# Flamingo block on one core: the last absorbed queries in another PSUM bank, and three steps of the second attention issued in another order

## The reference

```python
x = x + tanh(g_xattn[1]) * attention(layernorm(x), ctx_512, ...)

def attention(hidden_q, kv_c, Wq, w_kc_q, w_kc_kv, W_qr, W_kr, Wo):   # 16 heads, 1444 keys of 64
    q_big = rope(einsum('bshk,hkq->bshq', (hidden_q @ Wq.T).reshape(B, S, 16, 128), w_kc_q))
    kv_r = rope(kv_c)
    q_r = einsum('bshq,hqr->bhsr', q_big, W_qr)
    k_r = einsum('bld,hdr->bhlr', kv_r, W_kr)
    attn = softmax(einsum('bhsr,bhlr->bhsl', q_r, k_r))
    ctx_c = einsum('bhsl,bld->bhsd', attn, kv_r)
    ctx = einsum('bhsd,hkd->bhsk', ctx_c, w_kc_kv).transpose(0, 2, 1, 3).reshape(B, S, 2048)
    return ctx @ Wo.T
```

## Time and profile before

| | |
|---|---|
| profiled execution | 3362.52 us |
| its span, first to last instruction | 3360.6 us |
| granted TensorE clock, mean over the span | 0.935 |
| TensorE busy | 2867.2 us, 85% |
| VectorE busy | 2437.6 us, 73% |
| GpSimd busy | 1773.9 us, 53% |
| ScalarE busy | 1485.8 us, 44% |
| first group's first pair to the last group's last pair | 961.5 to 3076.2 us |

### The profile page before, as it was taken

The page is one execution under the profiler, slowest core; times in us unless marked ns, Lnnn a source line. Parts: engine busy times, 40 slices in busy tenths (PEclk is TensorE's granted clock), DMA queues, the critical chain, the costliest instruction groups (busy, mean ns, idle before and its releaser), DMA issues. The chain is left out here.

```text
span 3360.6 us, 61691 instructions
## 1 busy us (share of the span) xinstructions
PE 2867.2 (85%) x18352; PEld 1927.7 (57%) x18352; DVE 2437.6 (73%) x4098; ACT 1485.8 (44%) x3074; POOL 1773.9 (53%) x1268
## 2 busy tenths in 40 slices
PE   5999979999788998998998898899899899887345
PEld 4777769999554554564565555455456456554123
DVE  6877755444487787787777778778778777776887
ACT  2333322222155545545545545554554554544456
POOL 0000022222266766757676676776675667664566
PEclk9988879999799999999999999999999999998566
DMA  4000010000300100100000000000000000010100
GB/s 110 0 0 0 0 47 10 10 7 8 79 11 16 25 12 18 23 11 21 18 16 17 20 21 14 19 22 12 19 22 12 20 18 16 11 47 21 57 13 24
DMA packets 130244, 71.05 MB, mean 21 GB/s; under 512 B 83582, under 2 KB 124510, under 8 KB 129880
## 3 DMA queue, kind: packets, MB, share of 16 engines
q1 hardware_dynamic: 129944, 67.45, 8.1%
HBM read 56.95 MB, written 10.04 MB: 20 GB/s over the span
## 5 line engine op out<-in xcount | busy, mean ns | idle before, releaser
L1187 POOL TENSOR_TENSOR c_psum<-c_p 120x800 f32<-120x800 f32 (+1 forms) x384 | 752.5, 1963 | 487.4 <-ACT c_p L1471 277.7
L1471 ACT ACTIVATE c_p<-c_s_ps 120x400 f32<-120x400 f32 (+1 forms) x1536 | 657.2, 507 | 499.8 <-PE c_s_ps L1632 463.1
L1267 DVE TENSOR_REDUCE c_mpart<-c_m_ps 128x1 f32<-128x484 f32 x1080 | 655.8, 652 | 158.5 <-PE c_m_ps L1539 157.0
L1644 PE MATMUL c_o_ps<-c_p,c_val 120*64 120x400 f32 (+1 forms) x3072 | 609.7, 519 | 22.6 <-ACT c_onum L1438 11.4
L1539 PE MATMUL c_m_ps<-c_kmax,c_q 64*128 64x484 f32 x1080 | 324.8, 459 | 116.7 <-DVE c_mpart L1267 112.9
L1294 DVE TENSOR_TENSOR c_acc<-c_acc,c_psum 120x800 f32<-120x800 f32 x256 | 348.7, 1362 | 65.2 <-POOL c_psum L1187 63.1
L1178 POOL TENSOR_TENSOR l_rr<-c_psum,l_rr 96x400 f32<-96x400 f32 x256 | 260.8, 1040 | 192.3 <-DVE l_rr L1316 192.2
L1644 PEld LDWEIGHTS c_o_ps<-c_p,c_val 120*64 120x64 f32 (+1 forms) x3072 | 189.2, 137 | 276.0 <-issue 163.7
L1539 PEld LDWEIGHTS c_m_ps<-c_kmax,c_q 64*128 64x128 f32 x1080 | 144.6, 189 | 341.1 <-DVE c_mpart L1267 273.8
L1575 PE MATMUL c_s_ps<-c_xt,l_a 128*96 128x400 f32 x1536 | 311.2, 352 | 10.6 <-DVE l_rr L1316 8.1
L1628 PE MATMUL c_s_ps<-c_q,c_k 64*120 64x400 f32 (+1 forms) x1536 | 311.6, 369 | 2.6 <-ACT c_p L1471 2.6
(11 more groups left out here) (252 smaller groups left out, 5021.9 us busy)
## 6 DMA issues: line engine op xcount, KB each, us to landing
c_rdb<-l_denominators SPq DMA_DIRECT2D x128, 100.0 KB, 2.7
c_kv<-in_ctx SPq DMA_DIRECT2D x32, 360.0 KB
c_mrow<-c_mneg SPq DMA_DIRECT2D x288, 0.5 KB, 2.0
x_rows<-in_x SPq DMA_DIRECT2D x4, 800.0 KB
x_spill<-x_rows SPq DMA_DIRECT2D x8, 400.0 KB
l_xa<-x_spill SPq DMA_DIRECT2D x8, 400.0 KB
c_xr<-x_spill SPq DMA_DIRECT2D x32, 100.0 KB
x_spill<-c_xr SPq DMA_DIRECT2D x32, 100.0 KB
```

What stands on the lines that cost most here:

```text
L1187: g.tensor_tensor(psum[0:k, u % 2, :], p[0:k, 2 * u % 4, :], p[0:k, (2 * u + 1) % 4, :], ALU.add).then_inc(psum_ready, 1)
L1267: v.tensor_reduce(mpart[:, t, bank:bank + 1], m_ps[:, bank, 0:4 * KP], AX.X, ALU.max, negate=True).then_inc(mpart_ready, 1)
L1471: a.activation(p[0:k, w % 4, i * HALFQ:(i + 1) * HALFQ], s_ps[0:k, (2 * w + i) % 4, 0:HALFQ], ACT.Exp).then_inc(exp_ready, 1)
L1644: mm = pe.matmul(o_ps[i * DL:(i + 1) * DL, 0:HALFQ], val[0:k, j % 2, r, :], p[0:k, w % 4, i * HALFQ:(i + 1) * HALFQ], start=(r == 0), stop ...
```

## The change

Four edits, all in the second attention:

- The last pair of absorbed heads goes into bank 2 of `m_ps` and no longer into `o_ps`. The first values of the group wait for all but the last two entries of `q2`; the first unit in bank 2 (the third unit of the group, in slot 2) waits for all of `q2`. `absorb` waits for the maxima and for the residual that used bank 2.
- On SyncE `fold_denominators` goes ahead of a `load_combined`: for the chunk before in j = 1, and for the chunk in hand in j = 0 and 1. In j = 2 and 3 `load_combined(.., 6)` goes ahead of `write_inverses`.
- The first two steps of `rotate_keys` for batch b + 2 are issued after at = 7 and 8 of batch b, for j < 3; the third step follows after at = 0 of the next batch. The batch with j = 0 still does all three steps for b + 1 as well.
- `row_stats` goes from (c, q) = (0, 4) to (1, 0), `deviation` from at = 5 to 7, `normalise_rows` from (1, 0) to (1, 2), and `rows` from slot 17 to 20.

```diff
-            if (j, slot) == (G - 1, 17):
+            if (j, slot) == (G - 1, 20):
                 yield "rows", 0
...
                         load_combined(it, j, 4)
+                        if j == 1:
+                            fold_denominators(b * CH - 1)
                         load_combined(it, j, 5)
-                        if j > 0:
+                        if j > 1:
                             fold_denominators(b * CH - 1)
+                            load_combined(it, j, 6)
                         if j > 0:
                             write_inverses(b * CH - 1)
-                        load_combined(it, j, 6)
+                        if j < 2:
+                            load_combined(it, j, 6)
                         if j > 0:
                             spread_inverses(b * CH - 1)
...
                         if j + 1 < G:
                             load_combined(it, j + 1, 0)
+                        if j < 2:
+                            fold_denominators(b * CH)
+                        if j + 1 < G:
                             load_combined(it, j + 1, 1)
-                        fold_denominators(b * CH)
+                        if j >= 2:
+                            fold_denominators(b * CH)
                         write_inverses(b * CH)
...
                         if more or j + 1 < G:
-                            if at < 3:
+                            if j == 0 and at < 3:
                                 rotate_keys(b + 1, at)
+                            if j > 0 and at == 0:
+                                rotate_keys(b + 1, 2)
...
+                        if (more or j + 2 < G) and j + 1 < G and at in (7, 8):
+                            rotate_keys(b + 2, at - 7)
...
-                        if at == 5 and j + 1 == G and more:
+                        if at == 7 and j + 1 == G and more:
                             deviation(it + 1)
...
-                        if more and (j, c, q) == (G - 1, 0, 4):
+                        if more and (j, c, q) == (G - 1, 1, 0):
                             row_stats(it + 1)
-                        if more and (j, c, q) == (G - 1, 1, 0):
+                        if more and (j, c, q) == (G - 1, 1, 2):
                             normalise_rows(it + 1)
...
                         if n == first_in(2, 3 * NC0):
-                            pe.wait_ge(x_added, PRIMED + it * G)
+                            pe.wait_ge(q2_ready, PRIMED + (it + 1) * H)
...
                         if r == 0 and (j, c) == (0, 0):
-                            pe.wait_ge(q2_ready, PRIMED + (it + 1) * H)
+                            pe.wait_ge(q2_ready, PRIMED + (it + 1) * H - 2)
...
                             if what == "absorb":
-                                absorbed(it, False, H // 2 - 1)
+                                pe.wait_ge(mpart_ready, PRIMED + it * NMG + issued)
+                                pe.wait_ge(x_added, PRIMED + it * G)
+                                absorbed(it, False, H // 2 - 1, m_ps[:, 2, :])
```

More of the change, by code:

```diff
@@ L1294, in add_sums, with low_queries @@
                         v.tensor_tensor(acc[0:k, :], acc[0:k, :], psum[0:k, q % 2, :], ALU.add).then_inc(acc_ready, 1)
-                def low_queries(gi, pair):
+                def low_queries(gi, pair, src):
                     v.wait_ge(q1_ready, PRIMED + 4 * (gi * (H // 2) + pair + 1))
@@ L1302, in low_queries @@
                         side, at = h // 2 // 4, h // 2 % 4 * S
-                        v.tensor_tensor(q2[side * DL:(side + 1) * DL, :, h % 2, at:at + S], o_ps[rows, 0:T].rearrange("p (b s) -> p b s", b=G),
+                        v.tensor_tensor(q2[side * DL:(side + 1) * DL, :, h % 2, at:at + S], src[rows, 0:T].rearrange("p (b s) -> p b s", b=G),
                                         q1[rows, :, head_cols(2 * pair + half)].bitcast(F32), ALU.subtract).then_inc(q2_ready, 1)
@@ L1322, in head @@
                         if i >= 3 and i % 2 == 1:
-                            low_queries(gi, i // 2 - 1)
+                            low_queries(gi, i // 2 - 1, o_ps)
                         if prev and i == 3:
@@ L1350, in group @@
                             if u == 0 and half == 1:
-                                low_queries(it, H // 2 - 1)
+                                low_queries(it, H // 2 - 1, m_ps[:, 2, :])
                             if half == 0 and u > 0:
@@ L1407, in _, with copy_queries @@
             def _(a):
-                def copy_queries(gi, pair):
+                def copy_queries(gi, pair, src):
                     a.wait_ge(q_ps_ready, PRIMED + gi * (H // 2) + pair + 1)
@@ L1413, in copy_queries @@
                             a.activation(q1[half * DL:(half + 1) * DL, :, head_cols(2 * pair + i)],
[L1414 removed]
+                                         src[i * DL:(i + 1) * DL, 0:T].rearrange("p (b s) -> p b s", b=G), ACT.Copy).then_inc(q1_ready, 1)
                 def copy_keys(b):
@@ L1448, in head @@
                         if i >= 3 and i % 2 == 1:
-                            copy_queries(gi, i // 2 - 1)
+                            copy_queries(gi, i // 2 - 1, o_ps)
                         what, *at = beside_head(i)
@@ L1480, in group @@
                                 if what == "absorb":
-                                    copy_queries(it, H // 2 - 1)
+                                    copy_queries(it, H // 2 - 1, m_ps[:, 2, :])
                                 if what == "den":
@@ L1552, in project, with absorbed @@
                     mm.then_inc(f_ready, 1)
-                def absorbed(gi, prev, pair):
+                def absorbed(gi, prev, pair, dst):
                     n = gi * (H // 2) + pair
@@ L1564, in absorbed @@
                             i = 2 * pair + half
-                            mm = pe.matmul(o_ps[half * DL:(half + 1) * DL, 0:T], m.mqk[:, a, HEADS[i], :], rot[:, i % 4, a, :], start=(a == 0), stop=(a == 1))
+                            mm = pe.matmul(dst[half * DL:(half + 1) * DL, 0:T], m.mqk[:, a, HEADS[i], :], rot[:, i % 4, a, :], start=(a == 0), stop=(a == 1))
                     mm.then_inc(q_ps_ready, 1)
@@ L1582, in head @@
                         if i >= 3 and i % 2 == 1:
-                            absorbed(gi, prev, i // 2 - 1)
+                            absorbed(gi, prev, i // 2 - 1, o_ps)
                         what, *at = beside_head(i)
```

1 line of the change is left out of this document (removed).

## The result

The changed kernel takes 3316.19 us (median of 4 runs, 3314.58 to 3324.25) against 3363.58 for the kernel before (4 runs, 3351.69 to 3374.88): a ratio of 0.9864, 95% interval 0.9825 to 0.9903. The profiled execution took 3316.05 us with a span of 3314.2 and a mean granted clock of 0.932. Against the 3280 that was forecast, the sign is right and 81 us of gain came as 47. The busy engines are the same as before: the page of the kernel after has

What follows compares the result with a forecast made beforehand. TensorE was taken as busiest, standing still mostly for maxima VectorE had not taken. Terms 5.1 + 1.4 + 3.2 + 2.1 - 2.0 - 1.1 = 8.7 us, times 8, plus 11.2 for statistics: 80.8 gained, 3280 us; range 3238 to 3330.

Steps and rivals of the forecast that it cites:

- signs of being right: `invert` not awaiting the fold, `turn_keys` not awaiting `c_kva`, pair 43 near 6.9 us, pair 1 waiting 2.2 us before a unit.
- the clock in pair 10: TensorE's granted clock in pair 10 was to stay at 1.00 if the forecast was right.
- signs of being wrong: Pairs 9 to 13 above 24 us, GpSimd releasing exponentials at 8 to 11, or TensorE awaiting `c_xt` at the head.
- Fold ahead, j = 0: In j = 0, TensorE's 3.41 us wait and the half clock behind it go: 5.1 us a pass (3.4 to 5.4).
- Fold ahead, j = 1, pair 21: VectorE's remaining 1.7 us fold wait at pair 21 goes: 1.4 us a pass gained (1.1 to 1.7).
- Pair 15: In j = 1, 1.00 us from the fold, 0.7 and 0.4 from shorter additions: 2.1 a pass (1.0 to 2.7).
- Pair 27: In j = 2, the 2.25 us key wait and 1.0 of VectorE's delay go: 3.2 us a pass (2.2 to 3.8).
- Where the rotation goes: Steps moved after at = 7 and 8 lengthen VectorE's additions: 2.0 us a pass lost (0 to 5.5).
- Bank: At pair 1 the `low_queries` wait moves ahead of two units: 1.1 us a pass lost (0.3 to 2.0).
- Statistics: In pair 43, later statistics remove TensorE's wait for `c_onum`: 1.6 us in seven passes (1.4 to 1.7).
- The reorder in j = 2, 3, and the rows: SyncE's 2.0 us later inverses are hidden, and the statistics work moved to pairs 43 to 47 costs nothing.
- the rival in which VectorE takes it back: Moved steps cost their full 5.5 us and the bank 2.0 a pass: gain 46 us, time 3314, chance 0.16.

## Why the prediction was right in sign and too high in size

Its forecast was 10.1 us a pass (8.7 and 1.4 for the statistics); 5.95 came. Of its signs of being right, the wait of `invert`, that of `turn_keys`, pair 43 and the wait at pair 1 came as said; the clock in pair 10 did not stay at 1.00 (0.90 in the fifth pass, last rows below). One of its signs of being wrong came too: pairs 9 to 13 above 24 us (25.0). By its own steps:

- **Fold ahead, j = 0**: 5.1 forecast, 5.4 measured (26.75 to 21.30 with the folds alone), the half clock behind the wait gone with it. Right, wait and clock both.
- **Fold ahead, j = 1, pair 21**: 1.4 forecast. The early fold by itself measured between -0.7 (folds alone against before) and -0.4 (early against late, 22.4 against 22.0); in the kernel after, with the rotation moved as well, the stretch is 0.6 shorter than before. Wrong: the wait goes, the addition behind it moves into GpSimd's sum, and TensorE waits in pair 23 instead. The 1.7 us of VectorE's wait were counted as TensorE's, and what VectorE does next wasn't asked.
- **Pair 15**: of 2.1, the 1.0 of the fold came (13.79 to 12.82 with the folds alone). The 1.1 for shorter additions did not: the kernel after has 13.01. The addition of pair 14 did fall, from 1.70 to 0.99 us, but the next one, which was to become 0.4 shorter, rose from 1.43 to 2.47 (means of the passes): it now begins 0.26 us behind a sum of GpSimd.
- **Pair 27**: 3.2 forecast, 3.9 measured (11.78 to 7.87), just above the upper end of 3.8.
- **Where the rotation goes**: 2.0 forecast, about 4.7 measured (kernel after against the one with the rotation undone: pairs 9 to 13 +3.7, 33 to 37 +1.2, 14 to 16 +0.2, 21 to 25 -0.4). The 3.7 repeats (24.7 to 25.2 in four kernels with reads beside the additions and the fold early, 21.2 to 21.5 in seven without); the 1.2 is less sure, since pairs 33 to 37 take 21.0 to 21.8 in kernels with the old rotation; by means (22.0 in the five kernels with reads beside the additions, 21.3 in the other eight) it is 0.7. This is the largest term that was mis-sized. The bounds, 0 to 5.5, held it; the choice inside them did not. "About half of that may reach TensorE" was a guess: in pairs 9 to 13, where VectorE has units back to back, two lengthenings of about 1.5 and 1.2 us (2.53 and 2.14 against 0.99) became 3.7 us, more than their sum. Two things come on top. The additions behind them changed too: the five in that stretch take 2.5, 2.2, 2.1, 2.3 and 1.0 us (means), with the rotation undone 1.0, 1.0, 1.3, 2.6 and 1.0, and VectorE's busy time is 3.2 us longer (23.13 against 19.90). And TensorE, which waits for it, was granted 0.87 to 0.93 over the stretch in all eight passes, with the rotation undone 1.00 (mean PE busy 20.95 us against 19.35 for the same work).
- **Bank**: 1.1 forecast, 1.1 measured, with the wait of 2.06 us where it was said to stand (2.2). The parts are right in part by luck: at full clock pair 1 grew by 0.5 us (5.15 to 5.64; 0.4 forecast), but the clock fell there in seven of eight passes, not in half, and with the old wait it also fell, in one to five of the eight (the kernel before, the bank undone, the folds alone).
- **Statistics**: 1.6 forecast and 1.5 measured in pair 43, by another cause. The last pass, which served as the yardstick, lacks the statistics and also the rotation in j = 3; the prediction saw one of the two. The rotation alone gives it (6.97), the statistics alone do not (8.24).
- **The reorder in j = 2, 3, and the rows**: nothing, as said.

The size came out at that of the rival in which VectorE takes it back (3314), by its mechanism: additions longer under moved steps. That the number is so near is chance: its own terms (5.5 and 2.0 lost, all other gains as forecast) are not the measured ones (4.7 and 1.1), and pairs 15 and 21 fell short as well. The sum of the measured terms is 5.4 - 0.6 + 1.0 + 3.9 - 4.7 - 1.1 + 1.5 = 5.4 a pass, and 0.3 from pairs 38 to 42; the table has 5.95. That only 0.3 is left doesn't show that every term fits: by the terms pairs 21 to 25 would lose 0.2 and the table has 0.6 of gain, and pairs 0 to 3 would lose 1.1 where the table has 1.8, two misfits that nearly cancel. The rule of the Trainium skill (SBUF — State Buffer, Who interferes with whom) that the prediction weighed gave each addition under a moved step all of the rest of that step; the 2.53 us beside a step of 1.84 agree.

What stays open: how much of the longer pairs 33 to 37 is the port's, since they vary by 0.8 us among kernels with the old rotation; and what decides whether TensorE's clock falls in pair 1. Pairs 0 and 1 vary by 0.5 us between kernels with the same code there because of it. With the bank undone the wait in pair 1 is 1.36 us in passes two to seven, yet three of them take 5.15 us at full clock and three 6.2 to 6.6 us. Pair 1 of its fourth and fifth pass:

```profile
1771.75:1776.90 5.15, 3.79 (x26) 2.05 (x24) 3.61 (x6) 3.56 (x8) 4.77 (x3) 1.00 0.05 19
2037.42:2044.03 6.61, 5.25 (x26) 2.45 (x24) 3.60 (x6) 3.56 (x8) 6.23 (x4) 0.77 0.02 7
```

## What to carry to other kernels

Before a GpSimd instruction that reads SBUF is moved, lay it beside VectorE's instructions with two SBUF inputs: here each that it met took longer by up to the rest of it, and where VectorE was full (pairs 9 to 13), more than all of that reached the end. A wait that is removed lets the work behind it start earlier, so look at what it then meets; and a wait that an edit frees one consumer from may already stand ahead of another in the same queue. When an iteration without some work serves as the yardstick, list everything that it lacks.
